# 14-wide attention layers: the rows of negated maxima become rows of the score operands, written by GpSimd

## The reference

```python
attn = jnp.einsum('bqc,bkc->bqk', q * scale, k)
rel_h = jnp.einsum('bhwc,hkc->bhwk', r_q, Rh)
rel_w = jnp.einsum('bhwc,wkc->bhwk', r_q, Rw)
attn = attn.reshape(-1, WIN, WIN, WIN, WIN) + rel_h[..., None] + rel_w[..., None, :]
attn = jax.nn.softmax(attn.reshape(-1, N, N), axis=-1)
out = attn @ v
```

## Time and profile before

| | us |
|---|---|
| median of 3 runs | 625.48 |
| lowest, highest | 622.08, 629.93 |
| the profiled execution | 622.1 |
| its span | 620.3 |

### The profile page before, as it was taken

One profiled execution on the slowest core, in us unless ns is written; L12 is line 12 of the kernel. 1 busy time (PEld: TensorE's weight loads), 2 busy tenths in 40 slices (PEclk: granted clock), 3 DMA queues, 4 the chain that ended last, 5 costly groups with the idle time before them and its releaser, 6 DMA issues.

```text
span 620.3 us, 10103 instructions
## 1 busy us (share of the span) xinstructions
PE 536.3 (86%) x3864; PEld 380.2 (61%) x3864; DVE 293.7 (47%) x776; ACT 230.5 (37%) x453; POOL 127.6 (21%) x194
## 2 busy tenths in 40 slices
PE   7967989788989859888988998979889888889997
PEld 5635767576545345565666694556477767665676
DVE  4645776480225252645747461136567862800143
ACT  4304545623343215265454404333245644232110
POOL 7003010112004223162462216020030100210020
PEclk8989999999989869999999999999989996899999
DMA  6892655014215425725637107302816410200001
GB/s 165 201 191 56 139 109 216 2 25 114 64 39 128 82 55 122 175 69 123 155 85 194 73 0 165 78 21 60 197 29 144 114 64 1 64 2 1 0 1 51
DMA packets 21863, 55.39 MB, mean 89 GB/s; under 512 B 4560, under 2 KB 10248, under 8 KB 21688
## 3 DMA queue, kind: packets, MB, share of 16 engines
q1 hardware_dynamic: 21432, 54.65, 36.6%
q0 software_dynamic: 384, 0.10, 0.1%
HBM read 12.28 MB, written 0.79 MB: 21 GB/s over the span
## 4 chain that ended last, share of the span: by engine, by line
PE 62%; DVE 15%; SPq 8%; ACT 6%; DMA 4%; issue 4%; DVEq 0%; ACTq 0%
PE PS L1212 59%; DVE NM L1111 4%; DVE REL L1096 3%; DMA QA<-REL 2%; PE PS L1228 2%; SPq L728 2%; ACT HT L981 2%; SPq L720 2%; ACT REL L940 1%; SPq L738 1%; DMA PT<-in_qm 1%; DVE HL L1121 1%; SPq L676 1%; ACT OT L919 1%; DMA QA<-NR 1%
## 5 line engine op out<-in xcount | busy, mean ns | idle before, releaser
L1111 DVE TENSOR_REDUCE NM<-PS 98x2 f32<-98x392 f32 (+2 forms) x192 | 105.2, 568 | 91.6 <-PE PS L1212 90.3
L960 ACT ACTIVATE PT<-PS 98x392 f32<-98x392 f32 (+2 forms) x192 | 95.6, 519 | 72.4 <-PE PS L1212 70.8
L1212 PE MATMUL PS<-KA,QA 128*98 128x196 f32 (+3 forms) x432 | 89.1, 301 | 27.5 <-DVE NM L1111 22.5
L1212 PEld LDWEIGHTS PS<-KA,QA 128*98 128x98 f32 (+3 forms) x432 | 62.0, 182 | 55.5 <-DVE NM L1111 30.4
L1212 PE MATMUL PS<-QA,KA 128*98 128x196 f32 (+2 forms) x480 | 90.2, 289 | 6.3 <-ACT PT L960 1.8
L1212 PEld LDWEIGHTS PS<-QA,KA 128*98 128x98 f32 (+2 forms) x480 | 69.9, 183 | 20.4 <-issue 10.7
L1212 PE MATMUL PS<-XT,WQKV 128*96 128x512 f32 (+1 forms) x128 | 57.0, 697 | 11.8 <-ACT OT L919 7.4
L1212 PE MATMUL PS<-W,HT 128*128 128x192 f32 x288 | 48.7, 328 | 9.0 <-ACT HT L981 9.0
L1212 PE MATMUL PS<-XT,W 128*128 128x512 f32 (+1 forms) x144 | 52.8, 625 | 3.5 <-issue 3.4
L1212 PEld LDWEIGHTS PS<-W,HT 128*128 128x128 f32 x288 | 46.6, 190 | 14.0 <-ACT HT L981 14.0
L1212 PE MATMUL PS<-NR,SEL 128*98 128x392 f32 x144 | 52.3, 363 | 0.5 <-DVE NR L1133 0.5
(11 more groups left out here) (107 smaller groups left out, 694.6 us busy)
## 6 DMA issues: line engine op xcount, KB each, us to landing
QA<-QHL SPq DMA_DIRECT2D x36, 192.0 KB
KA<-KHL SPq DMA_DIRECT2D x24, 228.0 KB
QA<-REL SPq DMA_DIRECT2D x24, 224.0 KB
QA<-QHL SPq DMA_DIRECT2D x12, 384.0 KB
KA<-KHL SPq DMA_DIRECT2D x12, 384.0 KB
KA<-PT SPq DMA_DIRECT2D x12, 380.0 KB
QA<-REL SPq DMA_DIRECT2D x24, 128.0 KB
W<-in_w SPq DMA_DIRECT2D x3, 768.0 KB, 4.4
```

Source lines behind the costliest of these rows:

```text
L960: nc.scalar.activation(dst, src, ACT.Exp).then_inc(probs_done.sem, 1)
L1111: nc.vector.tensor_reduce(dst, src, AX.X, ALU.max, negate=True).then_inc(max_done.sem, 1)
L1212: return nc.tensor.matmul(dst, lhsT, rhs, start=start, stop=stop, skip_group_check=loose)
```

## The change

For layers 0 and 2, the rows of `QA` and `KA` are put in another order: rows 0 to 9 for maxima, 10 to 23 masks, 24 to 79 relative positions, 80 to 127 queries and keys. `KA`'s rows 0 to 9 are constants that pick the key's window or border group; `QA`'s are zero while a head's maximum products run (the mask array loads them with zeros, and 6 of the 12 heads, which reuse a place, need a memset by POOL). Then POOL casts `NR` into them, 784 columns for the inner windows and 240 for the border, and the score products are done with two products a unit. `SEL`, `HOT`, its load and the clearing of `NR` go. The first score product of a head waits for the casts (`rows_placed`); the first maximum product of heads 6 to 11 also waits for the memset (`rows_zeroed`); DVE's cast to `NR` waits for POOL's casts of two heads before, no longer for the scores of two heads before.

```diff
+            self.max_parts = 2 * (NB + 1)
+            self.mask_row, self.rel_row = self.max_parts, 24
+            self.qk_row = self.rel_row + 2 * parts * window
...
-        sp.dma_start(HOT[:, :], io["hot"]).then_inc(hot_in.sem, 16)
...
-                nc.gpsimd.memset(m["NM"][:, :, :], 0.0)
-                nc.gpsimd.memset(m["NR"][:, :, :].bitcast(F32), 0.0).then_inc(hl_zero.sem, 1)
+                nc.gpsimd.memset(m["NM"][:, :, :], 0.0).then_inc(hl_zero.sem, 1)
...
-            elif step == "maxT" and not L.pads:
+            elif step == "aug" and L.pads and i >= L.ring:
+
+                pool.wait_ge(*scores_psum.at(n, L.units * (i - L.ring + 1) - 1))
+                nc.gpsimd.memset(m["QA"][0:L.max_parts, 0, i % L.ring, :].bitcast(F32), 0.0)\
+                    .then_inc(rows_zeroed.sem, 1)
+            elif step == "maxT" and L.pads:
+
+                rows, src = m["QA"][0:L.max_parts, 0, i % L.ring, :], m["NR"][:, i % 2, :].bitcast(F32)
+                inner = src.rearrange("r (p q) -> r p q", p=2)[:, :, 0:HALF_IN]
+                pool.wait_ge(*maxT_done.at(n, i))
+                nc.gpsimd.tensor_copy(rows[:, 0:FIRST_EDGE].rearrange("r (b p q) -> r b p q", b=NB, p=2),
+                                      inner.unsqueeze(1).broadcast_to([L.max_parts, NB, 2, HALF_IN]))
+                nc.gpsimd.tensor_copy(rows[:, FIRST_EDGE:], src).then_inc(rows_placed.sem, 1)
+            elif step == "maxT":
...
-                    dve.wait_ge(*(scores_psum.at(n, L.units * (h - 1) - 1) if L.pads else max_row_at(L, h - 2)))
+                    dve.wait_ge(*(rows_placed.at(n, h - 2) if L.pads else max_row_at(L, h - 2)))
...
+                    if L.pads and h >= L.ring:
+                        pe.wait_ge(*rows_zeroed.at(n, h - L.ring))
...
-                if k == 0 and not L.pads:
-                    pe.wait_ge(*max_row_at(L, h))
+                if k == 0:
+                    pe.wait_ge(*(rows_placed.at(n, h) if L.pads else max_row_at(L, h)))
...
-                    if k == 0:
-                        pe.wait_ge(*maxT_done.at(n, h))
-                    rows = m["NR"][:, h % 2, :]
...
-                    last = mm(PS[0:size, bank, 0:wide], SEL[:, min(k, NB)].unsqueeze(1).broadcast_to([128, size]),
-                              rows, False, True, True)
```

More of the change, by code:

```diff
@@ L115, in key_constants @@
     hot = np.zeros((w, parts, 2, n), np.float32)
-    masks = np.zeros((L.max_row - L.mask_row, n), np.float32)
+    masks = np.zeros((L.rel_row if L.pads else L.max_row - L.mask_row, n), np.float32)
     ones = np.ones((L.rows - L.max_row, n), np.float32)
@@ L133, in key_constants @@
             place(j, y % w, x % w)
-            masks[b % 2 * 3 + window, j] = 1
+            masks[L.mask_row + b % 2 * 3 + window, j] = 1
+    for part in range(2):
+        for b in range(NB + 1):
+            masks[part * (NB + 1) + b, inner_keys(b) if b < NB else slice(FIRST_EDGE, n)] = 1
     j = FIRST_PAD
@@ L142, in key_constants @@
             if kw < real:
-                masks[WINDOWS, j] = 1
+                masks[L.mask_row + WINDOWS, j] = 1
             elif kh < real:
-                masks[WINDOWS + 1, j] = 1
+                masks[L.mask_row + WINDOWS + 1, j] = 1
             j += 1
-    return np.ascontiguousarray(np.concatenate([hot.reshape(-1, n), masks, ones]))
+    return np.ascontiguousarray(np.concatenate([masks, hot.reshape(-1, n)]))
 def query_masks():
-    m = np.zeros((LAYERS[0].max_row - LAYERS[0].mask_row, NT), np.float32)
+    first = LAYERS[0].mask_row
+    rows = np.zeros((LAYERS[0].rel_row, NT), np.float32)
+    m = rows[first:]
     for b in range(NB):
@@ L159, in query_masks @@
             m[WINDOWS + 1, j] = -BIG if window == 1 else 0
-    return m
+    return rows
 def edge_queries(k):
@@ L544, in _build @@
     maxT_done = count("maxT_done", [HEADS] * 3 + [0])
+    rows_placed = count("rows_placed", per(lambda L: HEADS if L.pads else 0))
+    rows_zeroed = count("rows_zeroed", per(lambda L: HEADS - L.ring if L.pads else 0))
     max_row_in = [count(f"max_row_in{p}", per(lambda L: 0 if L.pads else HALF), 16)
@@ L714, in _ @@
                 if L.pads:
-                    moves = [(m["QA"][0:3 * hd, 0, s, :], m["QHL"][mine, :, :])]
+                    moves = [(m["QA"][L.qk_row:L.rows, 0, s, :], m["QHL"][mine, :, :])]
                 else:
@@ L722, in _ @@
                 if L.pads:
-                    moves = [(m["KA"][0:3 * hd, 0, s, :], m["KHL"][mine, :, :])]
+                    moves = [(m["KA"][L.qk_row:L.rows, 0, s, :], m["KHL"][mine, :, :])]
                 else:
@@ L1358, in _ @@
                                   m["KA"][0:L.rows, 0, s, inner_keys(k, part)],
-                                  m["QA"][0:L.rows, 0, s, inner_keys(k)], part == 0, False, True)
+                                  m["QA"][0:L.rows, 0, s, inner_keys(k)], True, True)
                 elif k == NB:
@@ L1560, in _pack @@
     arrays["qm"] = query_masks()
-    arrays["hot"] = np.zeros((128, NB + 1), np.float32)
-    for b in range(NB + 1):
-        arrays["hot"][b::NB + 1, b][:2] = 1
     arrays["idn"] = np.eye(128, dtype=np.float32)
```

37 lines of the change are left out of this document (12 added, 25 removed).

## The result

| | before | after |
|---|---|---|
| median us | 625.88 | 634.56 |
| lowest, highest | 622.08, 629.93 | 633.44, 635.06 |
| profiled execution, span | 622.1, 620.3 | 635.1, 633.3 |

The ratio is 1.0135, 95% interval 1.0069 to 1.0201 (four runs each); a second measurement gave 1.0191 (1.0041 to 1.034). The change makes the kernel slower by some 9 us, where I forecast none.

The account below looks back on a forecast made before the run. PE was taken to bound heads 4 and 8, DVE heads 3, 6 and 7. Terms 0.7 - 1.1 + 0.2 - 0.2 gave -0.4 us, no change; 624.5 us was stated, between 622 and the 625.48 median, range 617 to 636.

Parts of the forecast that it names:

- 1, heads 2 to 4 and 6 to 8 (four steps): Hand-off delays head 7 by 0.54 us, then a round takes 4.05 against 3.68; head 8 starts 0.91 later, heads 3, 4 likewise.
- step 2: Heads 4 and 8: six selecting products of 0.18 us go, 1.1 us, cancelling the 0.91 us delay twice a layer.
- Step 3: Heads 5 and 9: the hand-off to heads 6 and 10 is hidden behind DVE's reductions, counted at nothing.
- step 4: Layer 0's tail, heads 10 and 11: last maximum product 0.3 us earlier, products with V 0.7 us later.
- Step 5: Layer 2's tail, at 1.2 GHz: head 10 gains about 1.6 us, the hand-off takes some 0.5 back, so -1.1.
- Step 6: Head 1: casts behind GpSimd's key split make the first score product 2.2 us late, covered by DVE; 0.1 us a layer.
- step 8: Start: one small load less, a queue slot of 0.43 us ahead of the masks, counted at -0.2 us.
- PE is not the bound everywhere: Its opposite was a rival: PE bounds everywhere, so 144 products at 0.18 us save 26 us, giving 596; chance 0.05.
- The clock: Rival: fewer products and more waits bring two or three more 1.2 GHz stretches at 2.7 us, 628 to 630; chance 0.12.
- Step 7: Zeroing the ten rows on GpSimd, six times a layer at under 1 us each, counted at nothing.
- The rule that I weighed: GpSimd and certain DVE SBUF operations take one port pair in turns; head 1's casts collide, sum about +1 us.
- The dear hand-off: Rival: at 2.6 us instead of 1.30, paid at five places a layer, the hand-off adds 13 us: 635; chance 0.13.

Follow-up runs that it names:

- e1: The change plus a filler product of the selecting product's size in every score unit, not waiting for the maxima: 634.4 us, ratio 1.008.
- e2: The change without GpSimd's casts and memsets and PE's waits for them, maxima not subtracted: 622.4 us, ratio 0.992.
- e5: The change without casts, memsets and their waits (maxima not subtracted), with a filler product in every score unit: 625.7 us, ratio 0.997.
- e4: The change with five casts, each unit waiting for its own, and the filler product in all heads but 4 and 8: 623.0 us, ratio 1.0007.
- e3: The change with five GpSimd casts, one for each unit, each unit waiting for its own: 632.6 us, ratio 1.0078.
- e8: The kernel before, with rows placed by GpSimd, by unit, only in heads 4, 8 and 10; selecting products kept elsewhere: 620.8 us, ratio 0.9882.
- e6: The change with the zeroing of the ten rows moved from GpSimd to ScalarE: 633.9 us, ratio 1.0152.
- e10: The change with the filler product in heads 0 to 9 and none in heads 10 and 11: 636.2 us, ratio 1.0123.
- e7: The kernel before, with rows placed by GpSimd, by unit, only in heads 4 and 8; selecting products kept elsewhere: 622.6 us, ratio 0.9982.

## Why the prediction was wrong

Its steps against the trace, profiled executions of before and after, length of a head's step from first score product to first score product:

| step of the sum | predicted | layer 0 | layer 2 |
|---|---|---|---|
| 1, heads 2 to 4 and 6 to 8 (four steps) | +1.82 | +3.02 | +2.63 |
| 2, heads 4 and 8 | -1.80 | -2.08 | -2.09 |
| 3, heads 5 and 9 | 0 | +0.73 | +0.54 |
| 4 and 5, tail | +0.7, -1.1 | +1.95 | -0.75 |
| 6, heads 0 and 1 | +0.1 | +1.49 | +1.47 |
| 8, start | -0.2 | -0.7 | |
| between the loops | 0 | +7.8 | |
| behind them | 0 | -1.0 | |

**What held.** The price of one hand-off. The casts took 829 and about 377 ns (predicted 0.83 and 0.37). Where the clock is full, the chain is as the prediction had it. Timeline of after, head 8:

```profile
100.08 0.39 DVE L1151 CAST NR<-PS 10x240 fp32r<-10x240 f32 x1
...
100.53 0.83 POOL L853 CAST QA<-NR 10x784 fp32r<-10x784 f32 x1 [3.17 <-DVE NR L1151]
...
101.32 0.38 POOL L855 CAST QA<-NR 10x240 fp32r<-10x240 f32 x1
...
101.75 0.42 PE L1230 MATMUL PS<-QA,KA 128*98 128x196 f32 x2 [0.35 <-POOL QA L855]
```

The hand-off was priced right: from NR's end (100.47) to the first score product it is 1.28 us, predicted 1.30. Step 2 to 3 grew by 0.53 (predicted 0.54), the steady round is 4.04 in e1 and 4.11 after in layer 2 (predicted 4.05), and heads 4 and 8 gained 1.02 to 1.06 us each. That PE is not the bound everywhere held as well: e2, with all 144 products gone for nothing, gained 0.8% and not 26 us. Its low clock is in that figure, but its step from head 7 to 8 in layer 0, at the full clock, took 3.62 us where before took 3.68, with six products fewer.

**Step that failed first: the clock was left out of the sum.** The sum let gains of 5.5 us and a hand-off of 5.3 cancel. The runs give 0 to 3.3 us of gain and 8.7 to 12.2 us of hand-off. The clock stood among the rivals at 0.12, as "two or three more" tails of 2.7 us. In place of that the heads got 60 us more at 1.2 GHz. A clock that differs over more than one stretch was also one of the prediction's own signs of being wrong, and it came. The argument against it was that layer 0 ran heads 9 and 10 at 1.00 "with the same waits". But it isn't the waits that matter most: the change takes 71 of some 625 products from each loop, and e2, without any new wait, has 60.4 us at 1.2 GHz in its heads, while e1, with the waits and the filler, has 31.7. At the falls themselves the traces don't show the cause, since before has the same gaps at full clock. I priced a removed product at the 0.18 us that it delays the next one, and at nothing where DVE is the bound. It had a second worth there: with it the clock stays higher. e5 against e2, e1 against the change and e4 against e3 all show that in the clock. In time the last pair shows it, by 9.5 us; e1 is no faster than the change, and e5 is 3.3 us slower than e2, since there the product's own cost stands against it.

At 1.2 GHz the terms above change too. A product costs nearly twice as much: in e8's layer 0 the starts in head 6 are 0.32 to 0.34 us apart at the low clock and 0.18 to 0.20 in head 7 at the full one. Steps that DVE had set then take longer, as e2's 4.41 us show. Step 3, which I had at nothing, cost 0.2 to 0.4 us a head. In head 5 of layer 0 about half of its 0.36 us is the clock (from the maximum product to head 6's first score product 0.42 us, 0.25 before); the rest arose ahead of the fall at 91.1, and answers to step 2, which gained more than I had counted. In step 4 six products that were to be bound by exps ran at half speed; head 10 to 11 took 6.27 us, 3.95 before. Step 5 predicted the right sign by the right reason, a tail already at 1.2 GHz.

**Step 7, the zeroing at nothing.** Memset and casts pushed the division into DVE's next cast of HL, which was held for 0.43 us at 94.09. Head 6 to 7 took 4.78 us; without the memset (e6) it is 4.36. Over both loops DVE's 24 HL casts took 224 ns on average in place of 174, 1.2 us in all, a small part of the 9. The rule that I weighed was the right one at the wrong place: I wrote that it "would leave the steady heads alone", because I looked at DVE's reductions from PSUM and not at the small cast between them.

**Step 6, head 1.** The casts stood behind the key split, as said: the split ends at 56.73 and the first score product comes at 57.88 in after. The cover held where the clock was nearly full: heads 0 and 1 in layer 0 take 17.37 us in e1, with 3.4 us at 1.2 GHz among it, and 17.84 before. The change has 14 us at 1.2 GHz there and takes 1.5 us more. The clock alone doesn't make that: e2, with 9 us at 1.2 GHz and no hand-off, takes 17.45; e10, with 10 us and the hand-off, 20.36. The shares aren't shown. There the weighed rule did come true in a run, the change again, with DVE's casts beside GpSimd's:

```profile
469.62 0.83 POOL L853 CAST QA<-NR 10x784 fp32r<-10x784 f32 x1
470.40 0.81 POOL L855 CAST QA<-NR 10x240 fp32r<-10x240 f32 x1
470.41 1.00 DVE L1092 CAST QHL<-XNOS 96x784 fp32r<-96x784 f32 x3
```

The second cast took 0.81 us instead of 0.38, and its like in layer 0 took 0.72. That is 0.8 us in both layers, where by the rule I had allowed 1.4; in the change's first profile all 24 took 0.38.

**The rivals.** The dear hand-off had the time right (635) and the reason wrong: its casts were as cheap as forecast. Of the 9 us lost, the four kernels with and without work and hand-off give the hand-off all of it and more, since the products that were to pay for it brought 3.3 us at most. By the line through the runs of before, its wait itself is about what I had counted, and the rest is the clock; that division is the estimate above and not shown.

**Left open**: what makes the clock fall at one gap of PE and not at another (86 to 91 us above); why the middle stretch, which is the same program, gets more time at 1.2 GHz (the profiles with the work kept in at least nine heads, e1, e4, e5, e7 and e8, have 325.7 to 327.9 us there); whether head 10 adds to the gain of e8; and the start, which varied from 45.4 to 49.1 us over all profiles, so that step 8 can't be told from it.

## What to carry to other kernels

A product taken from a TensorE that waits for another engine does not come free: price a removal there at 1.2 GHz as well as at 2.4, and compare the granted clock of whole stretches afterwards. Take work away first where TensorE has no gap, and where what replaces it is ready early; here that was heads 4 and 8, with head 10 in e8, the one kernel whose gain is clear of the noise. Compare two traces at the same place of the program, not at the same time. And when a slow GpSimd operation is moved in time, look at every small DVE copy within SBUF that it may now lie beside, not only at those of the bottleneck.

## What the runs showed of the hardware

- The run-to-run spread of this kernel, 617 to 634 us, goes with the granted clock of the run (0.929 to 0.969, correlation -0.94, 3.9 us for each 0.01). A profiled execution that happens to lie at 0.961, as that of before, is no middle of its kernel (median 0.948 over 65).
- A GpSimd CAST over 10 partitions takes 829 ns for 784 elements and 377 for 240, so the time goes by the elements in a partition and hardly by the partitions: 1032 ns for 1024 over 96. From its end to PE's start it is about 0.05 us.
- A DVE cast of 120 x 10 took 0.93 us (e1) and 0.99 us (e3) instead of 0.17 when a GpSimd TENSOR_TENSOR of 128 x 512 ran beside it; a GpSimd CAST 0.81 instead of 0.38 beside DVE's casts.
